# Gated linear attention: the first gate's running sum made by a scan on VectorE instead of by products on TensorE

## The chip, the core and the metric

The program runs on one core of a Trainium2 chip. Its engines are TensorE (PE: products), VectorE (DVE), ScalarE (ACT), GpSimd (POOL) and SyncE (SP, which only issues transfers here). The metric is the time of one execution on the device in microseconds (us); lower is better. The kernel before takes 1802.73 us (median of 3 runs, 1801.64 to 1806.15).

## The reference, cut to what matters

Four blocks follow one another over 4 sequences of 1024 tokens of 128 channels: window attention, a gated block, causal attention with a recurrent branch, and a mixture of experts. The change is in the second, gated block, with 8 heads of 64 dimensions and chunks of 64 tokens. In it, `_L0_ffn_ref` holds a chunked recurrence:

```
g = jnp.cumsum(gc, axis=1)                 # log gates, summed along each chunk of 64 tokens
g_last = g[:, -1]
qg = qc * jnp.exp(g)
kg = kc * jnp.exp(-g)
A = jnp.einsum('cthd,cshd->chts', qg, kg)  # then masked to s <= t
o_intra = jnp.einsum('chts,cshe->cthe', A, vc)
k_out = kc * jnp.exp(g_last[:, None] - g)
chunk_kv = jnp.einsum('cthd,cthe->chde', k_out, vc)
decay = jnp.exp(g_last)
S, o_inter = S * decay[..., None] + chunk_kv, qg_c @ S      # the scan over chunks
```

There are two gates. The first is a log sigmoid of a low-rank projection, divided by 16, summed over all tokens. The second belongs to 4 routed memories: its sum runs over those tokens only that the router sends to the same memory. Its sum is thus weighted by a matrix that differs from tile to tile.

## The kernel before, in words

The gated stage works on 32 tiles of 128 tokens (`TILES`), 8 to a batch (`NT`). The two sums are taken over a tile of 128 tokens, centred on its middle: `gate_sum` is a constant matrix of 128 x 130 numbers, the lower triangle less one half-tile, with two more columns for the decay from the middle to the tile's end and from its start to the middle, all divided by 16. Dimensions lie in 4 `PAIRS` of two heads, 128 rows each.

The order of work is written out by hand in `gla_order`. All engines walk the same list of items and do what is theirs, each in order, and wait for one another by semaphores. One round of the list belongs to tile i and to n = i + 1:

```
round_ = [("pair", i), ("half", n), ("sc", i, 0), ("sc", i, 1), ("k2x", n), ("mx", n), ("mask", i),
          ("sum", n, 0), ("kt", i), ("soft", n), ("fin", i - 1), ("sum", n, 1), ("qk1", n), ("vk", n),
          ("z", n + 1), ("routed", n), ("kv", i, 0), ("kv", i, 1), ("av", i), ("in", i, 0), ("in", i, 1),
          ("mid", n), ("gk", n + 1)]
```

What the steps are, with the lines of the kernel before:

- **z** (L1923): both gates of a tile projected, tokens in the rows of PSUM; two products of 512 columns from two different groups of 32 rows. ScalarE makes |z|, exp and log of it (L2020, L2022, L2024), and VectorE joins them to the log gates **gk** (L1971), of shape 128 x 2 x 512.
- **sum 0** and **sum 1** (L2206): 4 products each, of the first gate with `gate_sum` and of the second gate with `mixed`, which VectorE makes per tile (L2299). They turn the gates as well: dimensions come to lie in the rows. ScalarE takes exp of the sum and of its negative (L2462, L2464) and of the decay columns (L2469).
- **pair** (L2189, L2194): second queries of tile i and second keys of tile n. VectorE weighs the queries (L2311, `q2`), and takes the keys' maximum and difference (L2316, L2320).
- **sc** (L2232): scores; VectorE masks both halves (L2359, L2368). GpSimd makes the 4 routed copies of q2 (L2501) and adds the masked halves (L2494, the join).
- **mx** (L2169 to L2172), **kt** (L2219, keys turned; ScalarE copies, L2477), **soft** (VectorE, L2333 to L2337), **fin** (L2278, L2283; ScalarE L2484, L2487; VectorE L2388, L2394, L2398), **qk1** (L2212; VectorE L2344, L2346), **vk** (L2176, L2180; VectorE L2327, `k2`).
- **kv** (L2244, L2246; VectorE adds, L2379), **av** (L2258), **in** (L2270), and **mid**: a factor on VectorE (L2353), with which GpSimd decays the state (L2509) as soon as `in` has read the old one. `in` and `mid` are left out for the first tile of a batch.

Three pairs of PSUM banks form a ring: each item that needs one takes the next, and waits until the item three places before it has been read. `kv 1` thus waits for `vk`'s reader (L2327), and `pair` for `z`'s reader (L1971). Items of the next batch or of the next stage are put into the rounds by `beside`: statistics, norm, turns, routing, gates.

## Time and profile before

| | us |
|---|---|
| median of 3 runs | 1802.73 |
| the profiled execution | 1806.19 |
| its span | 1804.9 |
| TensorE busy | 1556.2 |
| VectorE busy | 1275.3 |
| ScalarE busy | 1098.3 |
| GpSimd busy | 697.8 |

The gated stage starts at about 278 us of the span, where its first z is issued, and ends at about 941 us. A row of a timeline gives start and length of an instruction (or of several that follow one another), engine, line, operation, names out<-in, shape and count, and in brackets how long the engine had been idle and what ended that. A product on 32-bit numbers stands as two instructions, so the 4 products of a sum are x8. An instruction that is held up after it has started shows it in its length, not as idle time.

### The profile page before, as it was taken

The numbers are of one execution on the slowest core, as the hardware profiler recorded it, in microseconds if no ns is written. First come the engines' busy times: TensorE is split into PE (matmuls) and PEld (weight loads), VectorE is DVE, ScalarE is ACT, GpSimd is POOL, SyncE is SP. The second block draws the span as 40 slices with busy tenths as digits, with TensorE's granted clock in tenths as the row PEclk, the third lists the DMA queues.
The fourth block names the chain that finished last, engine by engine and source line by source line (L and its number), as shares of the span: only waits on it lengthen the run. The fifth ranks groups of instructions, "written<-read, shape, count | busy, mean of one in ns | idle before, by whom it ended". The sixth has DMA issues, their size and how long they took to land. (4 is left out here: it accounts for less than half of the span.)

```text
span 1804.9 us, 45554 instructions
## 1 busy us (share of the span) xinstructions
PE 1556.2 (86%) x19648; PEld 998.5 (55%) x19648; DVE 1275.3 (71%) x2003; ACT 1098.3 (61%) x1641; POOL 697.8 (39%) x499
## 2 busy tenths in 40 slices
PE   3587897899999999999977778888788888899999
PEld 2354566787778778877863232433333343466565
DVE  4656644777777677768767868778777886655665
ACT  3255576777767777786752567677667767533331
POOL 4122300554255344534450556365465545411100
PEclk8789898999999999999997889999999999999999
DMA  7864200000000000000024274246237222223332
GB/s 176 196 165 113 47 5 12 2 2 2 2 2 2 2 1 2 2 1 2 32 88 99 52 212 98 63 133 142 56 107 167 66 64 72 67 71 94 95 96 76
DMA packets 54821, 121.17 MB, mean 67 GB/s; under 512 B 6124, under 2 KB 14468, under 8 KB 53020
## 3 DMA queue, kind: packets, MB, share of 16 engines
q1 hardware_dynamic: 51708, 112.74, 23.7%
q10 hardware_dynamic: 2912, 5.51, 1.8%
q8 instruction: 155, 2.54, 0.6%
q14 instruction: 46, 0.38, 0.1%
HBM read 85.70 MB, written 31.74 MB: 65 GB/s over the span
## 5 line engine op out<-in xcount | busy, mean ns | idle before, releaser
L1445 DVE TENSOR_REDUCE arena<-ring 128x2 f32<-128x1024 f32 (+2 forms) x320 | 342.1, 1110 | 87.9 <-PE ring L1302 62.1
L1545 ACT ACTIVATE arena<-ring 128x1024 f32<-128x1024 f32 (+1 forms) x320 | 291.3, 937 | 135.4 <-PE ring L1331 92.0
L1352 PE MATMUL accs<-arena 128*9 128x512 f32 (+3 forms) x1536 | 174.3, 528 | 3.8 <-ACT arena L1545 3.8
L2509 POOL TENSOR_TENSOR arena<-arena 128x1280 f32<-128x1280 f32 x28 | 65.3, 2332 | 287.0 <-PE accs L2270 231.7
L1295 PE MATMUL ring<-arena 48*128 48x512 bf16 (+3 forms) x768 | 128.8, 347 | 41.8 <-DVE arena L1445 21.1
L1324 PE MATMUL ring<-arena 51*128 51x512 bf16 (+3 forms) x768 | 125.0, 343 | 45.8 <-DVE arena L1445 25.1
L2501 POOL TENSOR_TENSOR arena<-arena 128x512 f32<-128x512 f32 x112 | 141.3, 1294 | 3.0 <-DVE arena L2311 3.0
L287 POOL TENSOR_SCALAR xn<-x,moments,rstd 128x128 f32<-128x128 f32 x80 | 65.0, 825 | 192.3 <-DVE rstd L258 178.3
L2782 ACT ACTIVATE arena<-ring 128x512 f32<-128x512 f32 x80 | 47.7, 596 | 134.8 <-PE ring L2651 132.7
L2494 POOL TENSOR_TENSOR arena<-arena 128x1024 f32<-128x1024 f32 x32 | 86.3, 2698 | 108.1 <-DVE arena L2368 108.1
L1718 POOL TENSOR_TENSOR arena<-arena 128x1024 f32<-128x1024 f32 x28 | 65.9, 2354 | 128.6 <-ACT arena L1558 104.5
L2742 DVE TENSOR_TENSOR arena<-arena,ring 128x512 f32<-128x512 f32 x80 | 54.9, 687 | 82.9 <-PE ring L2653 70.3
L1324 PEld LDWEIGHTS ring<-arena 51*128 51x128 bf16 x768 | 36.6, 95 | 137.9 <-DVE arena L1445 75.6
L2665 PEld LDWEIGHTS accs<-weights_large,arena 128*128 128x128 f32 x640 | 83.6, 193 | 37.9 <-issue 31.6
L1295 PEld LDWEIGHTS ring<-arena 48*128 48x128 bf16 x768 | 38.4, 96 | 110.3 <-DVE arena L1445 42.6
L2665 PE MATMUL accs<-weights_large,arena 128*128 128x128 f32 x640 | 85.3, 277 | 0.7 <-DVE arena L2748 0.7
L2454 ACT ACTIVATE arena<-arena 128x512 f32<-128x512 f32 x128 | 81.4, 707 | 0.0
L628 DVE TENSOR_REDUCE arena<-ring 128x8 f32<-128x1024 f32 x49 | 59.3, 1220 | 29.2 <-PE ring L521 29.0
L2246 PE MATMUL ring<-arena 128*64 128x256 f32 x512 | 76.0, 381 | 0.0
L1706 POOL TENSOR_TENSOR arena<-arena 128x1024 f32<-128x1024 f32 x32 | 75.5, 2360 | 0.1
L1455 DVE TENSOR_TENSOR_SCAN arena<-arena 128x1024 f32<-128x1024 f32 x32 | 73.8, 2306 | 2.3 <-POOL arena L1706 2.3
L2244 PEld LDWEIGHTS ring<-arena 128*64 128x64 f32 x512 | 36.1, 135 | 60.2 <-issue 30.6
(342 smaller groups left out, 4165.9 us busy)
## 6 DMA issues: line engine op xcount, KB each, us to landing
arena<-whole_k SPq DMA_DIRECT2D x32, 512.0 KB, 4.6
arena<-whole_q SPq DMA_DIRECT2D x32, 512.0 KB, 6.2
arena<-moe_scratch SPq DMA_DIRECT2D x128, 128.0 KB, 2.9
arena<-c_scratch_q SPq DMA_DIRECT2D x14, 384.0 KB, 9.3
arena<-c_scratch_k SPq DMA_DIRECT2D x14, 384.0 KB, 12.2
a_scratch_k<-arena SPq DMA_DIRECT2D x8, 512.0 KB, 4.2
c_scratch_k<-arena SPq DMA_DIRECT2D x8, 512.0 KB, 4.5
arena<-a_scratch_q SPq DMA_DIRECT2D x9, 384.0 KB, 7.2
```

What stands on the lines that cost most here:

```text
L1295: mm = nc.tensor.matmul(o[r], qs[half(r, SCORE), pair, n * P:(n + 1) * P], ks[half(r, SCORE), pair, a:c], start=True, stop=not diag)
L1324: mm = nc.tensor.matmul(o[r], ks[half(r, SHIFT), 2 * g + pair, j * P:(j + 1) * P], qs[half(r, SHIFT), 2 * g + pair, a:a + cols], start=Tru ...
L1352: mm = nc.tensor.matmul(acc[ci % 2][32 * h:32 * h + HD + 1, a - c * BANK:BANK], c_values[b % 2][:, j, r * HEADS // 2 + 2 * g + i, :], weig ...
L1445: nc.vector.tensor_reduce(dst, src, AX.X, ALU.max, negate=True).then_inc(c_max_taken.up(item), 1)
L1455: nc.vector.tensor_tensor_scan(sk[:, :], c_retain[:, j:j + 1].to_broadcast([P, T]), sk[:, :], 0.0, ALU.mult, ALU.add).then_inc(c_state_mad ...
L1545: nc.scalar.activation(view(c_probs[wi % 4]), view(ps), ACT.Exp).then_inc(c_weights_made.up(item), 1)
L1706: nc.gpsimd.tensor_tensor(sk[:, :], sk[:, :], c_vT[:, :], ALU.mult).then_inc(c_kv_made.up((b, j)), 1)
L2246: mm = nc.tensor.matmul(ps[r * GLA_D:(r + 1) * GLA_D, o + GLA_D:o + DENSE * GLA_D], k_nat[1][:, cols], v5[t % 2][:, 1:DENSE, cols], start= ...
L2454: nc.scalar.activation(v5[t % 2][:, 1 + r, :], v5[t % 2][:, 0, :], ACT.Copy, scale=route_hot[t // NT % 2][:, t % NT, r:r + 1]).then_inc(v_ ...
L2494: nc.gpsimd.tensor_tensor(masked[0][:, :], masked[0][:, :], masked[1][:, :], ALU.add).then_inc(gla_joined.up(t), 1)
L2501: nc.gpsimd.tensor_tensor(pair_cols(q2m[:, r, :]), pair_cols(q2[t % 2][:, :]), hot_b[t % 2][:, r * P:(r + 1) * P].unsqueeze(1).to_broadcas ...
L2665: mm = nc.tensor.matmul(moe_total(b, h)[:, n * P:(n + 1) * P], hid[i % 3][:, n * P:(n + 1) * P], w("d_down", f * P, (f + 1) * P), start=f ...
```

## The change

The first gate's z is projected turned: where one product gave 128 tokens x 512 dimensions, four products now give 128 dimensions x 128 tokens each, with the weights and the low-rank activations exchanged. The second gate's z is as it was, and is issued first. VectorE's gk is the same instruction. Right behind it VectorE now does three more for the first gate: the sum over the first half of each tile (`tensor_reduce` to 128 x 4), its subtraction from the first column (128 x 4), and a scan over 512 columns which `pair_keep` restarts at each of the 4 pairs. ScalarE takes both exps from that scan in SBUF, with the scale 1/16, and the two decays from the scan's last columns and from `gk_head`. The item `sum 0` has nothing left on TensorE and no place on the ring, so that every later item of a round sits one place further back.

```
@@ z, on TensorE
-                for i in range(2):
-                    rows = slice(64 * (1 - h) + 32 * i, 64 * (1 - h) + 32 * i + 32)
-                    mm = nc.tensor.matmul(ps[:, i * BANK:(i + 1) * BANK], low_of(b, h)[rows, 1, in_half(t)],
-                                          w("b_second", (1 + h) * BANK, (2 + h) * BANK)[rows, :], start=True, stop=True)
+                nc.tensor.matmul(ps[:, BANK:2 * BANK], low[rows[1], :], up_gates[rows[1], :], start=True, stop=True)
+                for p in range(PAIRS):
+                    cols = slice(p * P, (p + 1) * P)
+                    mm = nc.tensor.matmul(ps[:, cols], up_gates[rows[0], cols], low[rows[0], :], start=True, stop=True)
@@ gk, on VectorE
                 if t:
                     dv.wait_ge(sum_mm, (t - 1, 1))
+                    dv.wait_ge(sum_exp, (t - 1, 0, "decay"))
+                else:
+                    dv.wait_ge(gla_cleared, "pair first")
                 nc.vector.scalar_tensor_tensor(gk[:, :, :], z, 0.0, el[:, :, :], ALU.min, ALU.subtract)...
+                by_pair = gk[:, 0, :].rearrange("p (a c) -> p a c", a=PAIRS)
+                nc.vector.tensor_reduce(gk_head[:, :], by_pair[:, :, 0:P // 2], AX.X, ALU.add)...
+                nc.vector.tensor_tensor(by_pair[:, :, 0], by_pair[:, :, 0], gk_head[:, :], ALU.subtract)...
+                nc.vector.tensor_tensor_scan(gk[:, 0, :], pair_keep[:, :], gk[:, 0, :], 0.0, ALU.mult, ALU.add)...
@@ the ring, and sum on TensorE
-            on_ring = ("turn", "logits", "rows_hot", "rows_w", "low", "gate", "z", "mx", "vk", "sum", "qk1", "pair", "kt",
+            on_ring = ("turn", "logits", "rows_hot", "rows_w", "low", "gate", "z", "mx", "vk", "qk1", "pair", "kt",
-                    elif kind == "sum":
+                    elif kind == "sum" and item[2] == 1:
@@ sum 0, on ScalarE
+                    elif kind == "sum" and item[2] == 0:
+                        running = gk[:, 0, :]
+                        ac.wait_ge(z_step, (t, "running"))
+                        nc.scalar.activation(up[0][:, :], running, ACT.Exp, scale=1 / NORMALIZER)...
+                        nc.scalar.activation(dn[0][:, :], running, ACT.Exp, scale=-1 / NORMALIZER)...
+                        nc.scalar.activation(decay[t % 3][:, :, 0, 0], pair_cols(running)[:, :, P - 1], ACT.Exp, ...
+                        nc.scalar.activation(decay[t % 3][:, :, 1, 0], gk_head[:, :], ACT.Exp, scale=1 / NORMALIZER)...
@@ once, on GpSimd
+                nc.gpsimd.memset(pair_keep[:, :], 1.0)
+                nc.gpsimd.memset(pair_cols(pair_keep[:, :])[:, :, 0:1], 0.0)
```

On TensorE, a round of the first batch from the second scores to z, before. The names give the buffer of the ring that is written; L2206 is the sums, L2219 kt, L2278 and L2283 fin, L1923 z.

```order
L2232 MATMUL accs<-arena 128x128 x8
L2169 MATMUL ring2<-arena 128x128
L2170 MATMUL ring2<-arena 128x128
L2172 MATMUL ring2<-arena,bf_route_bcast 128x128 x4
L2206 MATMUL ring0<-weights_constants,arena 128x130 x4
L2219 MATMUL ring1<-weights_constants,arena 128x128 x8
L2278 MATMUL ring2<-arena,weights_constants 128x512
L2283 MATMUL ring2<-weights_large,arena 128x128 x4
L2206 MATMUL ring0<-arena 128x136 x4
L2212 MATMUL ring1<-xnT0,weights_large 128x128 x8
L1923 MATMUL ring0<-weights_large,arena 128x512 x2
```

The same round now (L2232 is kt, L2291 and L2296 fin, L2219 the sum that is left, L2225 qk1, L1925 and L1928 z):

```order
L2245 MATMUL accs<-arena 128x128 x8
L2186 MATMUL ring2<-arena 128x128
L2187 MATMUL ring2<-arena 128x128
L2189 MATMUL ring2<-arena,bf_route_bcast 128x128 x4
L2232 MATMUL ring0<-weights_constants,arena 128x128 x8
L2291 MATMUL ring1<-arena,weights_constants 128x512
L2296 MATMUL ring1<-weights_large,arena 128x128 x4
L2219 MATMUL ring2<-arena 128x136 x4
L2225 MATMUL ring0<-xnT0,weights_large 128x128 x8
L1925 MATMUL ring2<-weights_large,arena 128x512
L1928 MATMUL ring2<-arena,weights_large 128x128 x4
```

The four products behind mx are gone, kt follows at once, and from there on each item takes the ring buffer that its predecessor had. z has five products in place of two.

On VectorE, the end of a round and the start of the next, before: the two adds of kv, the factor, gk, and then the queries q2 and the keys of pair.

```order
L2379 TENSOR_TENSOR arena<-ring,arena 128x640 x2
L2353 SCALAR_TENSOR_TENSOR arena<-arena 128x20
L1971 SCALAR_TENSOR_TENSOR arena<-ring,arena 128x1024
L2311 SCALAR_TENSOR_TENSOR arena<-ring,arena 128x512
L2316 TENSOR_REDUCE arena<-ring 128x8
L2320 TENSOR_TENSOR arena<-ring,arena 128x512
```

And now, with the semaphores waited for (L1988 is the scan, under the name that it has in the instruction stream):

```order
L2392 TENSOR_TENSOR arena<-ring,arena 128x640 [waits kv_mm]
L2366 SCALAR_TENSOR_TENSOR arena<-arena 128x20 [waits sum_exp]
L1978 SCALAR_TENSOR_TENSOR arena<-ring,arena 128x1024 [waits sum_mm,z_act]
L1982 TENSOR_REDUCE arena<-arena 128x4 [waits z_step]
L1985 TENSOR_TENSOR arena<-arena 128x4 [waits z_step]
L1988 SCALAR_TENSOR_TENSOR arena<-arena 128x512 [waits z_step]
L2324 SCALAR_TENSOR_TENSOR arena<-ring,arena 128x512 [waits q2_routed,pair_mm]
L2329 TENSOR_REDUCE arena<-ring 128x8
```

Three instructions stand between gk and q2, each waiting for the one before it.

## Rows read from the trace of the kernel before

**Rows 1.** Busy time in the stretch 330 to 900 us: PE, PEld, DVE, ACT, POOL, clock.

```profile
330.00:900.00 570.00, 544.96 (x6916) 440.67 (x6916) 430.39 (x733) 420.57 (x740) 256.69 (x153) 1.00 0.01 4
```

**Rows 2.** Waits, 330 to 900 us: who for whom, total, times, longest.

```profile
PE ring L2244 <- DVE arena L2327: 13.2, 18, 1.2
```

**Rows 3.** Timeline of VectorE over one round: start, length, instruction, idle before.

```profile
501.07 0.69 DVE L2311 SCALAR_TENSOR_TENSOR arena<-ring,arena 128x512 f32<-128x512 f32 x1 [2.27 <-PE ring L2194]
...
503.00 1.21 DVE L2359 TENSOR_TENSOR arena<-ring,weights_constants 128x1024 f32<-128x1024 f32 x1
...
506.61 1.32 DVE L2337 SCALAR_TENSOR_TENSOR arena<-arena 128x512 f32<-128x512 f32 x1
...
508.23 2.47 DVE L2394 SCALAR_TENSOR_TENSOR arena<-arena,weights_large 128x512 f32<-128x512 f32 x1
...
514.37 0.68 DVE L2327 TENSOR_TENSOR arena<-ring,arena 128x512 f32<-128x512 f32 x1
...
517.40 1.22 DVE L1971 SCALAR_TENSOR_TENSOR arena<-ring,arena 128x1024 f32<-128x1024 f32 x1
520.90 0.69 DVE L2311 SCALAR_TENSOR_TENSOR arena<-ring,arena 128x512 f32<-128x512 f32 x1 [2.27 <-PE ring L2194]
```

**Rows 4.** Timeline of TensorE, the same round.

```profile
503.26 1.11 PE L2206 MATMUL ring<-weights_constants,arena 128*128 128x130 f32 x8
504.27 1.09 PE L2219 MATMUL ring<-weights_constants,arena 128*128 128x128 f32 x8
...
511.06 1.13 PE L1923 MATMUL ring<-weights_large,arena 32*128 32x512 f32 x4
...
515.20 0.34 PE L2244 MATMUL ring<-arena 128*64 128x64 f32 x4 [1.16 <-DVE arena L2327]
...
519.69 0.37 PE L2189 MATMUL ring<-weights_large,arena 64*128 64x128 f32 x1
```

**Rows 5.** Timeline of GpSimd, the same round.

```profile
500.11 2.33 POOL L2509 TENSOR_TENSOR arena<-arena 128x1280 f32<-128x1280 f32 x1 [9.54 <-PE accs L2270]
502.40 4.98 POOL L2501 TENSOR_TENSOR arena<-arena 128x512 f32<-128x512 f32 x4
507.32 2.83 POOL L2494 TENSOR_TENSOR arena<-arena 128x1024 f32<-128x1024 f32 x1
```

**Rows 6.** Timeline of VectorE with a short scan; then groups by form, with mean ns.

```profile
1670.43 0.42 DVE L1785 TENSOR_TENSOR_SCAN arena<-arena 128x128 f32<-128x128 f32 x1
...
L2333 DVE TENSOR_REDUCE arena<-arena 128x8 f32<-128x512 f32 x28 | 18.9, 675 | 0.0
...
L2710 DVE TENSOR_REDUCE arena<-arena 128x8 f32<-128x128 f32 x4 | 1.0, 239 | 0.0
...
L249 DVE TENSOR_TENSOR rstd<-rstd 128x8 f32<-128x8 f32 x4 | 0.6, 160 | 0.0
```

**Rows 7.** Timelines in the causal stage: a scan on VectorE, a small copy on GpSimd.

```profile
1083.29 2.27 DVE L1455 TENSOR_TENSOR_SCAN arena<-arena 128x1024 f32<-128x1024 f32 x1
...
1083.14 0.25 POOL L1695 TENSOR_TENSOR arena<-arena 128x32 f32<-128x32 f32 x1
1083.45 2.14 POOL L1697 CAST arena<-arena 128x32 bf16<-128x32 f32 x1
```

**Rows 8.** Timelines of ScalarE: the first sum's exps, same round as Rows 3.

```profile
504.41 0.60 ACT L2462 ACTIVATE arena<-ring 128x512 f32<-128x512 f32 x1 [0.17 <-PE ring L2206]
...
505.43 1.11 ACT L2477 ACTIVATE arena<-ring 128x512 f32<-128x512 f32 x2
```

**Rows 9.** Timelines behind a batch's first tile, VectorE and GpSimd.

```profile
479.56 1.22 DVE L1971 SCALAR_TENSOR_TENSOR arena<-ring,arena 128x1024 f32<-128x1024 f32 x1
482.04 0.69 DVE L2311 SCALAR_TENSOR_TENSOR arena<-ring,arena 128x512 f32<-128x512 f32 x1 [1.26 <-PE ring L2194]
...
479.72 2.33 POOL L2509 TENSOR_TENSOR arena<-arena 128x1280 f32<-128x1280 f32 x1 [13.73 <-DVE arena L2353]
```

**Rows 10.** Timeline of VectorE at kv of another round.

```profile
554.60 0.82 DVE L2379 TENSOR_TENSOR arena<-ring,arena 128x640 f32<-128x640 f32 x1 [1.66 <-PE ring L2246]
```

More of the change, by code:

```diff
@@ L1821, in build @@
         low_T = [carve([P, 2, BANK])]
-        assert used[0] <= SHARED_NEXT
+        assert used[0] <= SHARED_NEXT, (used[0], SHARED_NEXT)
         used[0] = 0
@@ L1842, in build @@
         xnT_1 = carve([P, T])
+        pair_keep, gk_head = carve([P, BANK]), carve([P, PAIRS])
         assert used[0] <= SHARED
@@ L1920, in gla_first_pe @@
                 pe.wait_ge(low_made, (b, h))
-                for i in range(2):
-                    rows = slice(64 * (1 - h) + 32 * i, 64 * (1 - h) + 32 * i + 32)
-                    mm = nc.tensor.matmul(ps[:, i * BANK:(i + 1) * BANK], low_of(b, h)[rows, 1, in_half(t)],
-                                          w("b_second", (1 + h) * BANK, (2 + h) * BANK)[rows, :], start=True, stop=True)
+                rows = [slice(64 * (1 - h) + 32 * i, 64 * (1 - h) + 32 * i + 32) for i in range(2)]
+                low = low_of(b, h)[:, 1, in_half(t)]
+                up_gates = w("b_second", (1 + h) * BANK, (2 + h) * BANK)
+                nc.tensor.matmul(ps[:, BANK:2 * BANK], low[rows[1], :], up_gates[rows[1], :], start=True, stop=True)
+                for p in range(PAIRS):
+                    cols = slice(p * P, (p + 1) * P)
+                    mm = nc.tensor.matmul(ps[:, cols], up_gates[rows[0], cols], low[rows[0], :], start=True, stop=True)
                 mm.then_inc(z_mm.up(t), 1)
@@ L2091, in gla @@
             for item in order:
-                if item[0] in on_ring or item[0] == "sc" and item[2] == 0 or (
+                if item[0] in on_ring or item[0] == "sc" and item[2] == 0 or item[0] == "sum" and item[2] == 1 or (
                         item[0] == "next" and item[1] in ("turn", "q", "k")):
@@ L2455, in act_program @@
                                                  scale=route_hot[t // NT % 2][:, t % NT, r:r + 1]).then_inc(v_made.up(t), 1)
[L2456 to L2459 removed]
+                    elif kind == "sum" and item[2] == 0:
+                        running = gk[:, 0, :]
+                        ac.wait_ge(z_step, (t, "running"))
                         if t:
[L2461 to L2466 removed]
+                            ac.wait_ge(qk_decayed, (t - 1, "k1"))
+                        nc.scalar.activation(up[0][:, :], running, ACT.Exp, scale=1 / NORMALIZER).then_inc(
+                            sum_exp.up((t, 0, "up")), 1)
+                        nc.scalar.activation(dn[0][:, :], running, ACT.Exp, scale=-1 / NORMALIZER).then_inc(
+                            sum_exp.up((t, 0, "down")), 1)
@@ L2467, in act_program @@
                         if t >= 3 and last_factor(t - 2):
                             ac.wait_ge(state_step, (last_factor(t - 2), "factor"))
-                        nc.scalar.activation(decay[t % 3][:, :, :, first:first + d],
-                                             v4[:, :, P:P + 2 * d].rearrange("p a (k d) -> p a k d", k=2),
-                                             ACT.Exp).then_inc(sum_exp.up((t, i, "decay")), 1)
+                        nc.scalar.activation(decay[t % 3][:, :, 0, 0], pair_cols(running)[:, :, P - 1], ACT.Exp,
+                                             scale=1 / NORMALIZER).then_inc(sum_exp.up((t, 0, "end")), 1)
@@ new lines, in act_program @@
+                        nc.scalar.activation(decay[t % 3][:, :, 1, 0], gk_head[:, :], ACT.Exp, scale=1 / NORMALIZER).then_inc(
+                            sum_exp.up((t, 0, "decay")), 1)
+                    elif kind == "sum":
+                        v4 = pair_cols(ps[:, :])
+                        ac.wait_ge(sum_mm, (t, 1))
+                        if t:
+                            ac.wait_ge(qk_decayed, (t - 1, "q2"))
+                        nc.scalar.activation(pair_cols(up[1][:, :]), v4[:, :, 0:P], ACT.Exp).then_inc(
+                            sum_exp.up((t, 1, "up")), 1)
+                        nc.scalar.activation(pair_cols(dn[1][:, :]), v4[:, :, 0:P], ACT.Exp, scale=-1.0).then_inc(
+                            sum_exp.up((t, 1, "down")), 1)
+                        if t >= 3 and last_factor(t - 2):
+                            ac.wait_ge(state_step, (last_factor(t - 2), "factor"))
+                        nc.scalar.activation(decay[t % 3][:, :, :, 1:1 + ROUTES],
+                                             v4[:, :, P:P + 2 * ROUTES].rearrange("p a (k d) -> p a k d", k=2),
+                                             ACT.Exp).then_inc(sum_exp.up((t, 1, "decay")), 1)
@@ L2489, in pool_program @@
             def pool_program():
+                nc.gpsimd.memset(pair_keep[:, :], 1.0).then_inc(gla_cleared.up("pair keep"), 1)
+                gp.wait_ge(gla_cleared, "pair keep")
+                nc.gpsimd.memset(pair_cols(pair_keep[:, :])[:, :, 0:1], 0.0).then_inc(gla_cleared.up("pair first"), 1)
                 for item in order:
```

33 lines of the change are left out of this document (14 added, 19 removed).

## The prediction

> **What bounds the kernel now.** First I read the busy times of the gated stage. From 330 to 900 us TensorE is busy for 545.0 of 570 us, at the full 2.4 GHz clock, VectorE for 430.4, ScalarE for 420.6 and GpSimd for 256.7 [rows 1]. That looks like a stage bound by TensorE, in which every product removed is time gained. The reader should distrust this: 25 us of idle time over some 28 rounds is 0.9 us a round, as much as the removed products take. So the second view is the waits: 18 times in that stretch TensorE waits at kv for VectorE's k2 (L2327), 13.2 us in all [rows 2]. In such a round TensorE's own work is not what counts.
>
> The third view is one round on three engines. q2 starts on VectorE at 501.07 and in the next round at 520.90 [rows 3]. Backwards from there: pair was issued at 519.69, in a row behind kv 1, av and in, which started at 515.20, 0.15 after k2 ended (514.37 + 0.68) [rows 3, 4]. And k2 is late because L2394 took 2.47 us, up to 510.70. It has two inputs in SBUF, and GpSimd ran the join until 507.32 + 2.83 = 510.15 [rows 3, 5]. GpSimd went from one instruction to the next since 500.11: the state's decay, the routed copies until 507.38, the join [rows 5]. It started at 500.11 because `in` had been done. So the loop that sets this round is: TensorE's in, GpSimd's 10 us, L2394, VectorE up to k2, then TensorE's kv 1, av, in. TensorE's first sum isn't in it.
>
> **What is removed on TensorE.** L2206 starts at 503.26 and kt at 504.27 [rows 4], 1.01 us for four products; I take 0.95, since the instructions overlap and it can be no more than the 1.01. In a round as above it buys nothing: TensorE arrives at kv earlier and waits longer. It counts where TensorE sets the round. I know those by VectorE waiting at kv for products: 1.66 us at 554.60 [rows 10], and the like in a second round of each batch, two in each of the first three batches, 6 in all. They gain 6 x 0.95 = 5.7.
>
> **z on TensorE.** Eight instructions of 128 columns took 1.01 us [rows 4], so one takes 0.12 and one of 512 columns about 0.45. z is four of the latter and took 1.13, not 1.8 [rows 4]: its two row groups run side by side. Now there are two instructions of 512 in one group and eight of 128 in the other, 0.9 us each side. I take no change; bounds -0.1 and +0.75 (one after the other: 8 x 0.12 + 2 x 0.45 = 1.86 against 1.1). Only where TensorE or z sets the round does it matter.
>
> **The ring.** With one item fewer, what follows kt waits for the first mask (L2359, ends at 504.21), and kt would end at 503.26 + 0.95 = 504.21 as well [rows 3, 4]. With the 0.15 that a wake-up took above, this costs 0.15 in rounds that TensorE sets, if at all: +0.5 over three of them.
>
> **What is added on VectorE.** The scan: 128 columns took 0.42 us and 1024 took 2.27 [rows 6, 7], so 2.07 ns a column and 0.42 + 384 x 0.00207 = 1.22 for 512. The reduce over 256 columns lies between 0.24 (128) and 0.68 (512) [rows 6]; on the line between them 0.39. The subtraction of 4 columns 0.16, as for 8 [rows 6]. With some 0.03 between instructions that wait for one another, 1.22 + 0.39 + 0.16 + 0.09 = 1.86 us, 32 times, 60 us in all; bounds 1.7 and 2.15. Where does it lie? gk starts at 517.40 and ends at 518.62, q2 starts at 520.90 after 2.27 idle, waiting for pair [rows 3]. The scan would end at 520.48, 0.4 us before q2: q2 isn't delayed, and nothing queued behind it. Should the three take over 2.28 us, each further tenth would go into every round.
>
> **What the scan holds up.** It does more than fill idle time. In the causal stage a copy on GpSimd of 32 columns, next to one that took 0.25, took 2.14: it began 0.16 behind a scan and ended with it, at 1085.59 against 1085.56 [rows 7]. The scan reads two SBUF operands; so GpSimd stood still until some 0.2 before the scan's recorded end. In the gated stage GpSimd starts the state's decay at 500.11, 0.96 before q2 [rows 3, 5]. The new scan will run from 1.6 to 0.4 before q2, and hold the decay until 0.6 before q2: 0.37 later than now (bounds 0.2 and 0.6). As the decay heads the loop of GpSimd, copies, join, L2394, k2, this is +0.37 in each round that the loop sets: the third, fourth and seventh of a batch, three times, and three rounds of the last batch; 12 x 0.37 = +4.4. The state's decay itself is wanted by `in` a round later and costs nothing there.
>
> The Trainium skill (SBUF — State Buffer, section "SBUF: two separate sides") has this as a rule: VectorE with two SBUF inputs and a GpSimd instruction that reads SBUF share one pair of ports, whichever starts first has it for the whole instruction, and the other fully blocks. The trace agrees for the scan, by the 2.14 us above. The rule speaks against this change, since by a count of idle time on VectorE alone these 4.4 us would be nothing.
>
> **Behind a batch's first tile** the order is the reverse. There gk waits for z (L1971 at 479.56, ends 480.78), q2 follows at 482.04, and GpSimd's decay starts at 479.72 and lasts to 482.05 [rows 9]. The reduce (one SBUF input; L2333 beside GpSimd's copies still took its 0.68 [rows 3, 6]) passes, but the subtraction and the scan have two inputs and wait for the decay: subtraction done at 482.0, scan from 482.03 to 483.25. q2 starts at about 483.2, 1.15 later than now. Queued behind it are mask and copies, and TensorE's second scores wait for it. 4 rounds x 1.15 = +4.6; bounds 0.6 (no port is held: gk's end + 1.86 = 482.64) and 1.5.
>
> **ScalarE.** Its first sum took from 504.24, when it was free, to 505.43, when it went on to kt [rows 8]: 1.19, of which 0.17 was waiting. Now it doesn't wait, but has one small activation more and reads SBUF. I take it as even; bounds -0.2 and +0.2, hidden, since L2394 waits for GpSimd and not for ScalarE. The two memsets on GpSimd run long before they are needed. At the very start of the stage gk(0) no longer has TensorE's sum behind it, but the scan takes its place: nothing. The other 10 rounds wait for things that don't move, I take nothing, within 0.2 each way.
>
> **The sum:** -5.7 + 0.5 + 4.4 + 4.6 = +3.8 us. The profiled execution took 1806.19 with a span of 1804.9, so its like would be 1810.0. That execution is 3.5 above the median of 1802.73; on the median the forecast is 1806.5, or +0.2%.
>
> **Rivals.**
>
> 1. *TensorE is the bound after all.* For it: 96% busy [rows 1]. Then all 32 rounds gain 0.95, 30 us, 1772. Against it: the 18 waits [rows 2]. 0.04.
>
> 2. *The shift lets VectorE in earlier.* L2337 is asked for at 506.61, in the last of four routed copies, and ends at 507.93, before the join (507.32 + 2.83 is 0.5 more than the decay's 2.33 for more numbers) [rows 3, 5]. So at a hand-over VectorE goes first. The four copies end 1.25 apart, the third at 506.13, less 0.2 for the hand-over 505.9. Were GpSimd over 0.7 late instead of 0.37, L2337 would slip in behind the third copy, L2394 (508.23) behind the fourth, and the join would come last, where av has time for it. L2394 would take 0.75 instead of 2.47, and the 12 rounds would lose up to 1.7 each, on average about 1.0: 12 less, so 4.6 + 0.5 - 5.7 - 12 = -12.6, 1790. Against it: 0.7 needs the three instructions to take 0.35 more than I find. 0.12.
>
> 3. *The scan doesn't hold GpSimd here.* Then +0.6 x 4 behind the first tiles, nothing in the 12 rounds, and 0.5 - 5.7: -2.8, 1800. Against it [rows 7]. 0.12.
>
> 4. *z gets slower.* If the five products no longer run side by side, +0.75 in the 6 rounds that TensorE sets and in the 4 where gk waits for z: 10 x 0.75 = +7.5 on top of the forecast, 1814. It decides from 0.2 on. For it: the long product is now issued first, with both its passes, and the small ones queue behind. Against it: pair's products from two row groups are issued in the same way, one behind another. 0.17.
>
> **How the numbers follow.** The forecast has 0.50, the rivals 0.04, 0.12, 0.12 and 0.17, and 0.05 is left for the rest. A change of less than 0.3%, 5.4 us, can hardly be told from none here: 1797.3 to 1808.1 is "the same". The forecast, with its bounds of +-4, falls there with 0.33, above with 0.13, below with 0.04; rival 3 falls there, 1 and 2 below, 4 above. Faster 0.21, the same 0.46, slower 0.33. The range runs from 1794 to 1815: it leaves out rival 1, most of rival 2, and a slice above rival 4.
>
> **What the profile after would show.** The 32 scans at 1.2 us each. GpSimd's decay at about 2.7 to 2.8 instead of 2.33 in most rounds, since the wait for the scan stands in its length. Behind a batch's first tile, a small subtraction of about 0.7 us, and q2 1.15 later behind gk. TensorE's waits at kv longer, about 1 us more in a round such as that at 515.20, and TensorE's busy time lower by 30 us with hardly a change in the time. z at 1.1 us from first to last. The forecast is wrong if L2394 takes 0.75 in rounds where it took 2.4 (rival 2), if the decay keeps its 2.33 (rival 3), or if z takes 1.8 (rival 4).

## The result, and the profile after

The changed kernel takes 1818.38 us (median of 6 runs, 1815.83 to 1819.80), the kernel before 1803.13 in the same comparison (6 runs, 1794.84 to 1810.79). The ratio is 1.0082, with a 95% interval of 1.0054 to 1.0110; a second comparison on another occasion gave 1817.55 against 1802.48, 1.0082 (1.0062 to 1.0103). So it is slower by 0.8%, some 15 us. 1806.5 had been forecast, with a range up to 1815: the sign of the sum was right, its size was not, and the time lies outside the range.

The profiled execution took 1817.53 us, with a span of 1816.2 against 1804.9 before: 11.3 us more. Busy times of the whole span:

```profile
PE 1540.2 (85%) x19584; PEld 993.7 (55%) x19584; DVE 1352.4 (74%) x2099; ACT 1098.7 (60%) x1673; POOL 710.6 (39%) x501
```

and of the stretch of [rows 1], in the same columns:

```profile
330.00:900.00 570.00, 520.82 (x6721) 429.29 (x6719) 492.26 (x808) 414.80 (x760) 267.46 (x153) 0.99 0.01 3
```

TensorE is busy for 24 us less in this stretch, and for 16 less in the whole span, not 30. The granted clock of the stretch is 0.99 where [rows 1] had 1.00.

The gated stage itself is 13.4 us longer, more than the whole span. Its first z is issued at 274.25 instead of 278.17, so the stage ahead of it, in which nothing was changed, happened to be 3.9 shorter in this execution; and the stage behind it starts at 951.16 instead of 941.72. That makes 676.9 us against 663.6. What lies behind, unchanged too, is 1.9 longer (865.0 against 863.2; in all twelve traces it lies between 863.1 and 867.1).

What was added stands as the prediction sized it (groups of the gated stage by form: busy time, mean ns of one, idle time before):

```profile
L1988 DVE TENSOR_TENSOR_SCAN arena<-arena 128x512 f32<-128x512 f32 x32 | 39.2, 1224 | 1.1
...
L1982 DVE TENSOR_REDUCE arena<-arena 128x4 f32<-128x256 f32 x32 | 13.4, 420 | 1.1
...
L1985 DVE TENSOR_TENSOR arena<-arena 128x4 f32<-128x4 f32 x32 | 7.9, 247 | 1.1
...
L2538 POOL TENSOR_TENSOR arena<-arena 128x1280 f32<-128x1280 f32 x28 | 74.9, 2673 | 283.2 <-PE accs L2283 229.3 <-DVE arena L2366 54.0
```

The scan's 1224 ns were forecast as 1.22 us, the reduce's 420 as 0.39. GpSimd's decay (L2509 before, L2538 now) has grown from 2.33 to a mean of 2.67.

The same round as in [rows 3], the third of its batch, now on VectorE:

```profile
503.25 0.69 DVE L2324 SCALAR_TENSOR_TENSOR arena<-ring,arena 128x512 f32<-128x512 f32 x1 [0.36 <-PE ring L2211]
...
510.63 2.64 DVE L2407 SCALAR_TENSOR_TENSOR arena<-arena,weights_large 128x512 f32<-128x512 f32 x1
...
516.95 0.68 DVE L2340 TENSOR_TENSOR arena<-ring,arena 128x512 f32<-128x512 f32 x1
...
519.87 0.82 DVE L2392 TENSOR_TENSOR arena<-ring,arena 128x640 f32<-128x640 f32 x1 [1.51 <-PE ring L2259]
520.69 1.22 DVE L1978 SCALAR_TENSOR_TENSOR arena<-ring,arena 128x1024 f32<-128x1024 f32 x1
...
522.60 1.23 DVE L1988 TENSOR_TENSOR_SCAN arena<-arena 128x512 f32<-128x512 f32 x1
```

and on GpSimd, with the decay of the next round as the last row:

```profile
502.29 2.73 POOL L2538 TENSOR_TENSOR arena<-arena 128x1280 f32<-128x1280 f32 x1 [9.54 <-PE accs L2283]
504.97 4.99 POOL L2530 TENSOR_TENSOR arena<-arena 128x512 f32<-128x512 f32 x4
509.92 2.80 POOL L2523 TENSOR_TENSOR arena<-arena 128x1024 f32<-128x1024 f32 x1
...
523.22 2.73 POOL L2538 TENSOR_TENSOR arena<-arena 128x1280 f32<-128x1280 f32 x1 [10.50 <-PE accs L2283]
```

The reader is to see the loop of [rows 5] with its new first link. The decay starts where it did against `in`, but it lasts 2.73: it stands still until the scan is over. The four copies and the join follow 0.4 later, and L2407 (L2394 before) is still held by the join, until 512.72 + 0.5. From q2 to k2 the round is 0.4 longer (503.25 to 516.95 is 13.70, [rows 3] have 13.30). From k2 to gk it is longer too, and for that nothing in the prediction stands: 3.74 us now, 3.03 before. On TensorE:

```profile
515.25 0.34 PE L2257 MATMUL ring<-arena 128*64 128x64 f32 x4 [1.69 <-DVE arena L2359]
515.41 0.61 PE L2259 MATMUL ring<-arena 128*64 128x256 f32 x4
516.01 1.16 PE L2259 MATMUL ring<-arena 128*64 128x256 f32 x4
517.77 0.49 PE L2257 MATMUL ring<-arena 128*64 128x64 f32 x4 [0.60 <-DVE arena L2340]
```

and the first wait of that place in the kernel before, beside the one in [rows 4]:

```profile
512.68 0.34 PE L2244 MATMUL ring<-arena 128*64 128x64 f32 x4 [0.49 <-DVE arena L2346]
```

Now the first four products of 256 columns take 0.61 us and the next four 1.16. One microsecond at a time, with the granted clock as the last but two of the columns (first the changed kernel, then the one before at the same work):

```profile
515.00:516.00 1.00, 0.75 (x11) 0.61 (x13) 0.86 (x6) 0.97 (x2) 0.00 (x0) 0.95 0.00 0
516.00:517.00 1.00, 1.00 (x10) 0.34 (x7) 1.00 (x5) 1.00 (x2) 0.00 (x0) 0.50 0.00 0
...
518.00:519.00 1.00, 1.00 (x11) 0.65 (x11) 0.36 (x1) 1.00 (x3) 0.00 (x0) 0.50 0.00 0
```

```profile
516.00:517.00 1.00, 1.00 (x20) 0.95 (x18) 0.42 (x1) 1.00 (x3) 0.00 (x0) 1.00 0.00 0
```

Before, TensorE had waited twice at kv, 0.49 us for k1 and 1.16 for k2 [rows 4]. Now it waits 1.69 for k1, since its four products are gone and the loop is later, and 0.60 for k2. Within a microsecond of the end of the first wait the clock is at 1.2 GHz, half of its 2.4, for some 3.5 us (in 519 to 520 it is back to 0.84). Half as many products are done in a microsecond (10, against 20).

**Where the 13.4 us are.** 3.6 of them lie ahead of the first q2, and are treated below. From there on, the length of a round is the distance from one q2 on VectorE to the next. 31 rounds take 624.37 us before and 633.03 after, 8.7 more. By the place of a round in its batch of eight:

| rounds | before | after | difference | times |
|---|---|---|---|---|
| first of a batch | 23.16 | 24.36 | +1.20 | 3 (the very first: +0.37) |
| second | 19.02 | 19.00 | -0.02 | 4 |
| third | 19.83 | 20.94 | +1.11 | 4 |
| fourth | 19.01 | 19.43 | +0.42 | 4 |
| fifth | 20.10 | 19.92 | -0.18 | 3 |
| sixth | 20.36 | 20.50 | +0.14 | 3 |
| seventh | 19.74 | 20.14 | +0.40 | 3 |
| eighth | 20.46 | 19.55 | -0.91 | 3 |
| fifth to seventh of the last batch | 57.88 | 58.17 | +0.40, -0.23, +0.12 | 1 each |

The last tile's own work behind the last q2 takes 1.1 us more (21.70 against 20.59), with the clock at 0.50 from 940 to 942. This isn't shown to come of the change: in the twelve traces that piece takes from 20.1 to 24.2 us, and the shortest belongs to the changed kernel with one of the fillers below.

**The start of the stage.** z, gk and q2 at the start, before and then now:

```profile
278.17 1.13 PE L1923 MATMUL ring<-weights_large,arena 32*128 32x512 f32 x4 [0.56 <-DVEq L225]
...
295.62 1.23 DVE L1971 SCALAR_TENSOR_TENSOR arena<-ring,arena 128x1024 f32<-128x1024 f32 x1 [3.70 <-ACT arena L2024]
296.76 0.68 DVE L2311 SCALAR_TENSOR_TENSOR arena<-ring,arena 128x512 f32<-128x512 f32 x1
```

```profile
274.25 0.69 PE L1925 MATMUL ring<-weights_large,arena 32*128 32x512 f32 x1 [0.56 <-DVEq L225]
...
293.38 1.22 DVE L1978 SCALAR_TENSOR_TENSOR arena<-ring,arena 128x1024 f32<-128x1024 f32 x1 [3.75 <-ACT arena L2041]
...
296.43 0.67 DVE L2324 SCALAR_TENSOR_TENSOR arena<-ring,arena 128x512 f32<-128x512 f32 x1
```

From the first z to the first q2 it was 18.59 us and is 22.18. Between gk and q2 nothing had been waited for before (1.14 us); now VectorE's three instructions stand there in full (3.05), +1.91. The other 1.7 lie ahead of that gk: TensorE is idle for 5.34 us instead of 3.19 at its first remaining sum, and then the granted clock is 0.50 longer, so that qk1 takes 3.38 us instead of 2.18.

### The profile page after: what moved, and what is told of

Read it like the earlier page. It is cut to its first block and busy times, and to the rows that moved or that the text cites. A ratio compares the mean times of both kernels' runs of the same rounds, so it can differ in the third digit from the quotient of the medians.

```text
span 1816.2 us, 45524 instructions
## 1 busy us (share of the span) xinstructions
PE 1540.2 (85%) x19584; PEld 993.7 (55%) x19584; DVE 1352.4 (74%) x2099; ACT 1098.7 (60%) x1673; POOL 710.6 (39%) x501
## 5 line engine op out<-in xcount | busy, mean ns | idle before, releaser
L2538 POOL TENSOR_TENSOR arena<-arena 128x1280 f32<-128x1280 f32 x28 | 74.9, 2673 | 283.2 <-PE accs L2283 229.3
L2259 PE MATMUL ring<-arena 128*64 128x256 f32 x512 | 80.7, 398 | 0.0
L2407 DVE SCALAR_TENSOR_TENSOR arena<-arena,weights_large 128x512 f32<-128x512 f32 x32 | 68.1, 2129 | 9.1 <-ACT arena L2513 8.6
## 6 DMA issues: line engine op xcount, KB each, us to landing
arena<-c_scratch_k SPq DMA_DIRECT2D x14, 384.0 KB, 13.2
```

## The experiments

Three theories were to be told apart. The first: the added instructions cost by way of the port that VectorE and GpSimd share, in the loop rounds and behind the first tiles. The second: VectorE simply has more to do. The third: the removed products bring less than was thought, since TensorE's clock falls where it now waits longer.

**The scan with one operand.** The scan gives place to a reduce of the same length that reads one operand. This kernel leaves out the first gate's running sum.

```diff
-nc.vector.tensor_tensor_scan(gk[:, 0, :], pair_keep[:, :], gk[:, 0, :], 0.0, ALU.mult, ALU.add)
+nc.vector.tensor_reduce(pair_keep[:, 0:2 * PAIRS], gk[:, :, :].rearrange("p i (a c) -> p (i a) c", a=PAIRS),
+                        AX.X, ALU.add)
```

> The changed kernel with the scan replaced by a sum over both gates: as long on VectorE (a reduction of 1024 columns, 1.22 us), but with one SBUF operand; the first gate's sum is left out. Theory 'held up' (the scan stops GpSimd, whose loop of decay, copies and join sets 12 rounds): those rounds lose their 0.40 us each, the wait of TensorE in the third rounds gets shorter and its clock stays at full speed there, together 6 to 9 us below the changed kernel; behind a batch's first tile nothing changes, since the small subtraction still has two operands and waits. Rival 'VectorE time' (60 us more on VectorE, whatever its operands): the same time as the changed kernel, within 2 us.

Measured: 1808.16 us against 1800.81, 1.0046 (1.0030 to 1.0063). Its reduce lasts as long as the scan, but the decay is back at its old length (groups of the gated stage):

```profile
L2538 POOL TENSOR_TENSOR arena<-arena 128x1280 f32<-128x1280 f32 x28 | 65.3, 2331 | 286.6 <-PE accs L2283 232.6 <-DVE arena L2366 54.0
...
L1988 DVE TENSOR_REDUCE arena<-arena 128x8 f32<-128x1024 f32 x32 | 39.0, 1220 | 1.1
```

The fourth rounds take 19.01 again, the seventh 19.74: as before the change, to a hundredth. So it is not the time on VectorE that costs the 0.40. I put it down to the second operand; the reduce also differs from the scan in writing 8 columns and not 512, and no run separates the two. The fifth rounds take 19.51, so the loop's delay had also taken 0.4 of their gain. The first rounds stay at 24.35, because the subtraction still has two operands. By the rounds it would be near the kernel before, but for three (a third of the second and of the third batch, a second of the last) that lose 0.52, 1.46 and 1.62 us with the clock at 0.50 behind kv. That part of the expectation, full speed there, didn't hold. By the two ratios the kernel is some 6.5 us below the changed one, as forecast, and not within 2.

**Only what is added**, in the kernel before, with the result written where nothing reads it:

```diff
+nc.vector.tensor_reduce(gk_head[:, :], by_pair[:, :, 0:P // 2], AX.X, ALU.add)
+nc.vector.tensor_tensor(gk_head[:, :], by_pair[:, :, 0], gk_head[:, :], ALU.subtract)
+nc.vector.tensor_tensor_scan(gk_spare[:, :], pair_keep[:, :], gk[:, 0, :], 0.0, ALU.mult, ALU.add)
```

> The kernel before with the three VectorE instructions added (into spare memory, so nothing waits for them), and TensorE's first sum and z as they were. Theory 'held up': rounds that GpSimd's loop sets are 0.40 longer (12 of them), the first-tile rounds 1.2 (4), those that TensorE sets don't move: 8 to 10 us above the kernel before. Rival 'TensorE side' (the turned z, the shorter ring or the lower clock is what costs): within 2 us of the kernel before.

Measured: 1818.78 us against 1800.81, 1.0101 (1.0083 to 1.0119). The added instructions alone cost 1.0%. The fourth, seventh and first rounds are as long as in the changed kernel (19.40, 20.12, 24.35); the fifth and eighth have their old 20.11 and 20.46. The third rounds take 20.20, that is +0.37 as predicted and without the clock's share, except for one: 21.87 in the third batch. (In all, the 31 rounds take 13.2 us more, not 8 to 10: besides that one, the very first round takes 25.80 instead of 23.61, with the clock at 0.50 in its first five microseconds (293 to 298), and three sixth rounds 20.88 instead of 20.36, which I can't explain.) TensorE at kv in the second batch's third round and in that one:

```profile
513.95 0.34 PE L2258 MATMUL ring<-arena 128*64 128x64 f32 x4 [0.87 <-DVE arena L2360]
516.47 0.34 PE L2258 MATMUL ring<-arena 128*64 128x64 f32 x4 [1.15 <-DVE arena L2341]
...
678.47 0.34 PE L2258 MATMUL ring<-arena 128*64 128x64 f32 x4 [0.88 <-DVE arena L2360]
680.99 0.34 PE L2258 MATMUL ring<-arena 128*64 128x64 f32 x4 [1.15 <-DVE arena L2341]
```

and the clock in each, a microsecond behind the second wait:

```profile
517.00:518.00 1.00, 1.00 (x19) 0.91 (x17) 0.21 (x2) 1.00 (x3) 0.00 (x0) 1.00 0.00 0
...
682.00:683.00 1.00, 1.00 (x11) 0.75 (x10) 0.00 (x0) 1.00 (x3) 0.00 (x0) 0.50 0.00 0
```

The waits are the same to a hundredth, and the clock fell in one of the two. Two waits of about a microsecond are a place where it may fall, not one where it must.

**Only what is removed**: the changed kernel without the three instructions. It leaves out the first gate's running sum.

```diff
-nc.vector.tensor_reduce(gk_head[:, :], by_pair[:, :, 0:P // 2], AX.X, ALU.add)
-nc.vector.tensor_tensor(by_pair[:, :, 0], by_pair[:, :, 0], gk_head[:, :], ALU.subtract)
-nc.vector.tensor_tensor_scan(gk[:, 0, :], pair_keep[:, :], gk[:, 0, :], 0.0, ALU.mult, ALU.add)
...
-ac.wait_ge(z_step, (t, "running"))
+ac.wait_ge(z_step, (t, "gk"))
```

> The changed kernel without the three VectorE instructions; ScalarE reads the unsummed gates, so the first gate's sum is left out. Theory 'held up': only rounds that TensorE sets gain, 3 us or 5 us in all, less what a longer wait and a lower clock in the third rounds take back (up to 3 us): 1 to 5 us below the kernel before. Rival 'TensorE side': above the kernel before. Rival 'TensorE is the bound': 30 us below it.

Measured: 1801.26 us against 1800.81, 0.9995 (0.9979 to 1.0010): no gain that can be measured. By the rounds there is one, and it is taken back. The fifth rounds gain 0.58, the eighth 0.91, the very first 0.87, two of the last batch 0.64 and 0.30: 6.3 us. Four rounds lose, 0.50, 1.63, 1.33 and 2.41: 5.9 us. They are a second and three third rounds, all ones in which TensorE waits at kv, and the granted clock is 0.50 in each. In the second round of the second batch, on TensorE, 2.3 us behind a first wait of 0.73:

```profile
485.54 0.41 PE L2247 MATMUL ring<-arena 128*64 128x64 f32 x4 [0.91 <-DVE arena L2330]
485.68 1.12 PE L2249 MATMUL ring<-arena 128*64 128x256 f32 x4
```

and the clock there:

```profile
487.00:488.00 1.00, 1.00 (x9) 0.75 (x7) 0.09 (x1) 1.00 (x3) 0.00 (x0) 0.50 0.00 0
```

In this kernel no scan holds anything up, and the clock falls all the same. In the third rounds the wait for k1 is 0.49 us before, and no clock falls; 0.87 with what is added alone, one of four falls; 1.29 with what is removed alone, three of four (two of four in the kernel with the one-operand reduce, with the same wait); 1.69 in the changed kernel, and all fall, eight in two traces. So two thirds of the longer wait are the removal's and a third is the scan's, and the longer wait goes with the fall. Products that were gone from rounds in which TensorE waits didn't buy nothing, they cost.

**Products put back as filler.** To test this, the changed kernel has work added on TensorE ahead of kt in the third rounds, whose result is overwritten.

```diff
+if t % NT == 2:
+    for p in range(PAIRS):
+        nc.tensor.transpose(ps[:, p * P:(p + 1) * P], k1[t % 2][:, p * P:(p + 1) * P], ident)
```

> The changed kernel with four more transposes (0.95 us, a repetition of kt's first four, into the same place) in the third round of each batch. Theory 'clock' (TensorE waits so long for k1 in that round that it is granted 1.2 GHz afterwards, which costs 0.7 us): in those four rounds the granted clock stays at 2.4 GHz, kv takes 0.6 instead of 1.1 us, and the round is 20.2 instead of 20.9 us, though TensorE has more to do; 3 us less in all. Rival (the longer round comes from the delay of k1 and k2 alone): the same 20.9.

Measured: 1821.07 us against 1802.5, 1.0093 (1.0063 to 1.0122), and the third rounds still take 20.83 to 20.95. The test was too weak, and its expectation wrong in a size: the four transposes took some 0.44 us, not the time of the removed products, and the wait for k1 went only from 1.69 to 1.48. The clock fell again (TensorE at kv; the clock behind it was 0.50):

```profile
508.58 0.34 PE L2260 MATMUL ring<-arena 128*64 128x64 f32 x4 [1.48 <-DVE arena L2362]
```

**A longer filler**: kt's eight transposes done three times in those rounds; in the trace the last eight start 1.75 us later by it.

```diff
+if t % NT == 2:
+    for i, k_ in ((0, k1[t % 2]), (1, k2[t % 2])) * 2:
+        for p in range(PAIRS):
+            nc.tensor.transpose(ps[:, i * BANK + p * P:i * BANK + (p + 1) * P], k_[:, p * P:(p + 1) * P], ident)
```

> The changed kernel with kt's eight transposes issued three times in the third round of each batch: 1.9 us more for TensorE (the four extra of the first try took only 0.44 us, and the wait for k1 was still 1.48 us). Theory 'clock': TensorE then waits about 0.4 us for k1 instead of 1.69, the granted clock stays at 2.4 GHz in those rounds, and they take 20.2 us instead of 20.93, with more work. Rival (the length comes from the delay of k1 and k2 alone): 20.9 again, or more.

Measured in one execution, 1815.78 us. A single time says little beside the 16 us over which the kernel before spreads, but the rounds in the trace say what was asked. All four third rounds take 20.23 to 20.25, 0.70 less than in the changed kernel, with 1.75 us more to do on TensorE. At kv:

```profile
516.22 0.34 PE L2262 MATMUL ring<-arena 128*64 128x64 f32 x4 [0.19 <-DVE arena L2364]
...
518.74 0.34 PE L2262 MATMUL ring<-arena 128*64 128x64 f32 x4 [1.16 <-DVE arena L2345]
```

and the clock behind the second wait:

```profile
519.00:520.00 1.00, 1.00 (x18) 0.84 (x16) 0.33 (x1) 1.00 (x3) 0.00 (x0) 1.00 0.00 0
```

What is left of the third rounds' 1.11 is +0.40, the loop's own. The clock is thus shown to be 0.70 x 4 = 2.8 us of the stage. (One first round of this execution took 25.79 instead of 24.37. There too the granted clock is 0.50, from 637 to 640, behind a wait of 1.69 us for ScalarE.)

**The scan ahead of the decay behind a first tile.** There the decay is made to wait for the scan, so that VectorE's three instructions find the port free.

```diff
+if t % NT == 1:
+    gp.wait_ge(z_step, (t + 1, "running"))
```

> The changed kernel with GpSimd's decay behind a batch's first tile waiting until the scan is done. Theory 'held up' (there the subtraction and the scan wait for the decay, 2.33 us): subtraction 0.17 instead of about 0.7 us, q2 0.55 to 0.6 us earlier behind gk, and the four rounds before it 23.8 instead of 24.36 us. The decay itself comes 3 us later, and if its followers (routed copies, join) are then late, the next round gets longer than 19.00 by up to 1.5 us. Rival (VectorE's own three instructions are the whole 1.2 us): 24.36 as before.

Measured in one execution, 1824.71 us: against what was expected, no gain. VectorE and GpSimd behind the second batch's first tile:

```profile
481.48 0.17 DVE L1985 TENSOR_TENSOR arena<-arena 128x4 f32<-128x4 f32 x1
...
482.82 0.67 DVE L2324 SCALAR_TENSOR_TENSOR arena<-ring,arena 128x512 f32<-128x512 f32 x1
...
483.04 2.33 POOL L2540 TENSOR_TENSOR arena<-arena 128x1280 f32<-128x1280 f32 x1 [16.83 <-DVE arena L1988]
```

The subtraction takes 0.17 and that round 23.72 instead of 24.36 (the same in the third batch, 23.42 instead of 23.98 in the first, but 25.30 in the fourth). But the decay, and with it GpSimd's loop, starts 3.2 us behind gk (479.8) instead of 0.2, and the next round takes 22.13 instead of 19.00 (20.73 to 23.15 in the four batches). The price was moved, and grew. Not all of it is the late decay: TensorE waits 2.2 to 2.7 us at kv in these rounds, and in all four the granted clock falls to 0.50. This trace also has a third round, in the first batch, with the changed kernel's wait for k1 (1.68) in which the clock does not fall. It takes 20.21 us, which is the changed kernel's 20.94 less the same 0.7.

**The join made to wait.** Both kernels, the changed one and the one before, with the join held back until VectorE has scaled the output (L2394, L2407), which it otherwise blocks. It is wanted only by av, later.

```diff
 gp.wait_ge(gla_masked, (t, 1))
+if t:
+    gp.wait_ge(o_scaled, (t - 1, "scaled"))
 nc.gpsimd.tensor_tensor(masked[0][:, :], masked[0][:, :], masked[1][:, :], ALU.add)
```

> The changed kernel with one wait more on GpSimd: the join of a tile waits until VectorE has done L2407 (the scaled output of the tile before). Theory 'held up': L2407 takes 0.75 us instead of 2.4 in most rounds, k2 comes up to 1.9 us earlier, GpSimd no longer sets any round and most become TensorE's: some 10 us less in each batch, 40 us below the changed kernel, about 1778. Rival 'VectorE time': VectorE still has its 60 us more and the wait moves to another of its instructions: less than 10 us gained.

> The kernel before with the same wait more on GpSimd (the join waits for the scaled output of the tile before). Theory 'held up': TensorE's own work then sets nearly all rounds, its first sum included: about 5 us less in each batch, 20 us below the kernel before, about 1783, and so some 5 to 10 us above the changed kernel with the same wait. Rival 'VectorE time': below the changed kernel with the same wait, as it was without it.

Measured: the changed kernel with it 1789.29 us against 1800.81, 0.9938 (0.9917 to 0.9959), the kernel before with it 1792.89 against 1802.50, 0.9946 (0.9925 to 0.9968). The mean length of L2407 falls from 2129 ns to 747, and the join starts behind it (groups by form: join and L2407):

```profile
L2525 POOL TENSOR_TENSOR arena<-arena 128x1024 f32<-128x1024 f32 x32 | 89.0, 2782 | 124.5 <-DVE arena L2407 96.9 <-DVE arena L2381 27.6
...
L2407 DVE SCALAR_TENSOR_TENSOR arena<-arena,weights_large 128x512 f32<-128x512 f32 x32 | 23.9, 747 | 9.5 <-ACT arena L2513 8.9
```

and in a timeline of VectorE and GpSimd:

```profile
516.65 0.74 DVE L2407 SCALAR_TENSOR_TENSOR arena<-arena,weights_large 128x512 f32<-128x512 f32 x1
...
517.53 2.79 POOL L2525 TENSOR_TENSOR arena<-arena 128x1024 f32<-128x1024 f32 x1 [1.55 <-DVE arena L2407]
```

The loop as the prediction drew it is thereby shown: take the join off L2407, and the 31 rounds go from 633.03 to 607.95 us, and in the kernel before from 624.37 to 613.24. Here the change itself is a gain in the trace, 5.3 us in the rounds and 5.7 in the span (1787.3 against 1793.0), though the medians, 3.6 apart, don't tell the two kernels from each other with any certainty. Both gains are well short of what was expected, 29 us by the medians against 40 for the changed kernel, and 10 against 20 for the one before. In two of its four third rounds the clock still falls: they take 20.90 and 20.85, the others 19.28 and 19.29, behind the same wait of 1.98 us.

**Both waits**, the join's left out in the seventh rounds, which it had made longer (20.33 against 20.14):

```diff
-if t:
+if t and t % NT != 6:
     gp.wait_ge(o_scaled, (t - 1, "scaled"))
...
+if t % NT == 1:
+    gp.wait_ge(z_step, (t + 1, "running"))
```

> The changed kernel with both waits on GpSimd: the join behind L2407, except in the seventh round of a batch, where that round had become 0.2 us longer, and the decay behind the scan in the first-tile rounds. Theory 'held up': 1 us below after_join_later by the seventh rounds and 2 us by the first-tile rounds, about 1786, 0.9% below the kernel before, and below the kernel before with the join later (1793). Rival 'VectorE time': no lower than after_join_later.

Measured: 1790.54 us against 1802.48, 0.9939 (0.9919 to 0.9960), the same as with the one wait. The first rounds gain, 22.60 against 23.23, and the second lose, 18.44 against 17.32, so the 1786 expected weren't reached. With the join's wait alone the changed kernel beats both kernels without it, by 0.6% and by 1.4%. The kernel before with the same wait and the kernel with both waits can't be told from it by their times.

**The changed kernel again**, in the comparison of the last kernels:

> The changed kernel itself, once more beside the kernel before on one chip, to see how much of the 15 us between the medians (11 between the two profiled executions) is the change: by the rounds of the trace 9 to 12 us slower.

Measured: 1817.55 us, 1.0082 (1.0062 to 1.0103), 8.6 us more in the 31 rounds, and each place in the batch as in the table to 0.02 us. The whole stage takes 678.6 us here, 15.1 more than before: from the first z to the first q2 it is 23.03, and behind the last q2 22.62. The third rounds take 20.93 or 20.94, all four, so what is told of them isn't one execution's chance.

## Why the prediction was wrong

**What was forecast for the loop held; three terms failed.** Forecast was +3.8 us in the stage, measured +13.4. Two terms had been put at nothing: the stage's start (+3.6) and TensorE's longer waits (+2.8). A third, the gain of the rounds that TensorE sets, was too large by 1.9 us. Term by term:

- *The scan holds the decay*: 0.37 forecast in 12 rounds, +4.4. Measured 0.40 (the decay's 2.73 against [rows 5]) in 12 rounds, four third, four fourth, three seventh and one of the last batch: +4.9. The reduce with one operand gives it all back, which refutes rival 3. The rule of the Trainium skill (SBUF — State Buffer, section "SBUF: two separate sides") was right for the scan. It has whichever starts first hold the other, and the trace agrees in both directions: here the scan held GpSimd's decay (2.73 us instead of 2.33), in the next point the decay holds VectorE.
- *Behind a first tile*: 1.15 forecast in four rounds, +4.6. Measured 1.20 in three and 0.37 in the very first, +4.0. (By its own steps, with the scan until 483.25, the prediction should have had 1.24 and not 1.15. The very first round would gain 0.87 by the removal alone, as the kernel without the three instructions shows.) The steps are as they were drawn; on VectorE, and the decay on GpSimd:

```profile
480.56 1.22 DVE L1978 SCALAR_TENSOR_TENSOR arena<-ring,arena 128x1024 f32<-128x1024 f32 x1
...
482.26 0.81 DVE L1985 TENSOR_TENSOR arena<-arena 128x4 f32<-128x4 f32 x1
...
484.25 0.67 DVE L2324 SCALAR_TENSOR_TENSOR arena<-ring,arena 128x512 f32<-128x512 f32 x1
...
480.72 2.33 POOL L2538 TENSOR_TENSOR arena<-arena 128x1280 f32<-128x1280 f32 x1 [13.72 <-DVE arena L2366]
```

  A subtraction of four columns takes 0.81 us, because it ends with the decay that runs from 480.72 to 483.05, and q2 starts 3.69 behind gk instead of 2.48 [rows 9].
- *The rounds that TensorE sets*: -0.95 forecast in six, -5.7, with +0.5 for the ring in three of them. The eighth rounds gave -0.91 each. The fifth gave -0.18 each, and that is the mis-sized term: -3.3 in place of -5.2. TensorE does wait for a buffer of the ring there, but not behind kt and not because the ring is shorter. z waits for k1, qk1's reader. In the fifth rounds the gates' projection (L1916, L1915 before) stands between qk1 and vk, so that qk1 is three places ahead of z in both kernels:

```profile
554.88 0.68 DVE L2359 TENSOR_TENSOR arena<-ring,arena 128x512 f32<-128x512 f32 x1
...
555.62 0.69 PE L1925 MATMUL ring<-weights_large,arena 32*128 32x512 f32 x1 [0.60 <-DVE arena L2359]
```

  Before, k1 had ended at 551.45, ahead of z at 552.14. With the products gone VectorE's k1 is what comes last, and k1 is late by the same 0.40 as everything in GpSimd's loop: with the scan gone, or with one operand, these rounds gain 0.58. The prediction had counted the loop's delay in the loop's own rounds alone.
- *ScalarE as even*: the first sum takes from 546.67 to 547.90, when ScalarE goes on to kt, 1.23 us in that round against 1.19 in the round of [rows 8]. This held.

- *"The other 10 rounds wait for things that don't move"*, nothing: the second rounds -0.02, the sixth +0.14, two of the last batch -0.23 and +0.12. This held, some +0.2 in all.
- *"At the very start of the stage ... the scan takes its place: nothing."* This step failed, by +3.6 us. At the start nothing else is under way behind which the three instructions could lie. The second gk is followed by q2 1.14 us later before and 3.05 now; the kernel with what is added alone has the 3.05, the one with what is removed alone the 1.14. These 1.9 us are thus shown. The other 1.7, ahead of that gk, go with TensorE's longer idle time and lower clock there, and no run separates them: with what is added alone the way from the first z to the first q2 is 20.57 us, with what is removed alone 17.80, and in the kernels with both, the two traces of the changed one and its variants, 21.8 to 23.0.
- *"In a round as above it buys nothing: TensorE arrives at kv earlier and waits longer."* This step failed too. It does arrive earlier and wait longer, and a longer wait wasn't free: the clock falls to 1.2 GHz, and what stands behind kv runs at half the speed on the path that sets the end. In the third rounds this is 0.70 x 4 = 2.8 us (shown by the longer filler). In the kernel without the scan it took back nearly all that the removal had gained, 5.9 of 6.3 us. The profile before had the evidence that a price was possible: 18 waits up to 1.2 us at kv [rows 2], each one to be made longer by a microsecond. At kv it showed no fall, but at the stage's start, where TensorE had been idle for 3.19 us, it did:

```profile
284.00:286.00 2.00, 1.99 (x9) 2.00 (x10) 1.89 (x5) 0.07 (x1) 0.00 (x0) 0.50 0.00 0
```

  The prediction put no bound on such a price.

Together: 4.9 + 4.0 - 3.3 + 0.2 + 2.8 = 8.6, the 8.7 of the 31 rounds but for rounding. With the 3.6 ahead of the first q2 and the 1.1 behind the last, of which the latter may be chance, this is the stage's 13.4.

**The rivals.** 1 (TensorE is the bound) is refuted by the time. 2 (the hand-over flips) didn't occur, L2407 takes 2.64, but the join's wait brings about by design what it described, and -12 us was its price; measured are -11.1 us in the rounds of the kernel before and -25.1 in those of the changed one. 3 is refuted. 4 is refuted: z takes from 555.62 to about 556.7, 1.1 us as before.

**What isn't settled.** The medians differ by 15 us (9.7 to 19.8 by the interval). The stage is 13.4 and 15.1 us longer in the two traces of the changed kernel, so the change in the stage can account for all of it; but the kernel before has a single trace, and its own executions spread over 16 us. Nor is it shown what decides whether the clock falls: the same two waits were followed by either.

## What to carry to other kernels

Removing work from an engine that then waits longer on the path isn't free by itself: look at the granted clock behind the engine's waits, and give a longer wait a price before calling it cover. Count an added VectorE instruction with two SBUF operands against GpSimd's timeline as well as VectorE's own, in both directions, and then follow its delay into each round that the held chain touches, not only those that the chain already sets. Look at the start of a stage by itself: what hides behind other work in a full round stands there in full. And where a join on GpSimd is wanted late but runs early over a VectorE instruction on the path, one wait on the order of the two was worth more on the changed kernel (1.4%) than the whole change cost (0.8%). The same kind of wait on the decay, which is wanted early, cost time.

## What was not expected of the hardware

- TensorE's clock went to 1.2 GHz in the midst of a stretch granted 0.99 on average, around the end of a wait of 1.3 to 2.7 us or behind two of 0.7 to 1.3, and came back some 3 to 4 us later (three times, in two traces, after some 7). It was regular in the changed kernel (eight third rounds in two traces) and irregular elsewhere: behind waits of 0.87 and 1.15 us in one of four rounds, behind a wait of 1.98 us in two of four.
- A subtraction of four columns took 0.81 us instead of 0.17, waiting for a GpSimd instruction that had begun 1.5 us before it.
